# A six-sweep graph kernel on one core: DVE operands in PSUM, groups written out, indices resident, one-hots built in both orientations

## The chip, the cores and the metric

The kernel runs on one core of a Trainium2 chip, in float32 (some one-hots in bfloat16). The metric is the device time of one execution in microseconds, the lower the better: the median of three runs of the kernel before is 7284.38 us. The engines are named as in the profile: PE (TensorE matmul), PEld (its weight loads), DVE (VectorE), ACT (ScalarE), POOL (GpSimd) and SP (SyncE, which here issues only DMAs).

## What is computed

A graph has 3125 nodes with 128 channels and 100000 edges, sorted by destination. Six message-passing layers run one after the other, each over all edges:

```python
e = leaky_relu(el[src] + er[dst])              # L0, GAT, 8 heads: no vectors of the destination
alpha = (q[dst] * (k[src] + e_edge)).sum(c)    # L1, twice, 4 heads; e_edge = edge_attr @ We
alpha = (q[dst] * k[src]).sum(c)               # L2, 4 heads
e = (att * leaky_relu(xl[src] + xr[dst], 0.2)).sum(c)   # L3, twice, 8 heads
p = exp(alpha - segment_max(alpha, dst)[dst])
out = segment_sum(p * v[src], dst) / segment_sum(p, dst)
```

L0 also makes the edge attributes of L1: cos(relative time * Wt + bt) in 64 channels beside 64 given ones. Between the layers stand projections, norms, a feed-forward part and residual sums per node.

## The kernel before

`edge_sweep` runs once per layer, with the kinds "gat", "tconv" (twice), "mha" and "gatv2" (twice). Edges lie in tiles of 128, one edge per partition; 8 tiles are a group, and a sweep has 98 groups (the last has 6 tiles with edges and 2 of padding). Buffers are rings of S = 4 slots (`rows`, `qwin`, `neg`, `part`).

For each group POOL issues 8 indirect DMAs (`gather`, L739), one per tile, each of which fetches 128 rows of the source node's table (1 KB a row in tconv and mha, 512 B in gatv2, 576 B in gat) into `rows`, with its indices read from `idx`, which ACT has cast from `src_col` (L760). POOL's only waits are for `idx` and for the messages of the group four earlier. SP loads 8 windows of 128 destination rows (`qwin`, L674), the marks for the segment maxima (`neg`, L678) and, in tconv, the edge attributes (L680), and stores the partial sums (`part_tab`, L703), 8 runs of 544 or 576 bytes per partition.

A tile's destinations are numbered by rank within the tile. `hot` is the one-hot [edge, rank] and `hot_t` its transpose. In gat and mha DVE builds the one-hot (L981); in tconv and gatv2 ACT does (L780: |rank - column| tile by tile, L791: relu(1 - gap)). PE transposes it (L883), ACT copies it out of PSUM to `hot_t` (L766) and, outside gat, casts `hot_b` to `hot` (L774). PE spreads the destination rows over the edges with `hot_t` (L902, and L899 for edge attributes), DVE forms the scores (`scores`: L1030 adds the edge term to k and v, L1040 multiplies; in gatv2 L1033 adds, L1036 is the slope as max(0.2x, x), L1037 multiplies by att; L1042 reduces), PE transposes the scores (L917), DVE takes running maxima in two scans (L988, L992) and the difference (L997), ACT takes the exponent (L798), PE transposes maxima and weights back (L909, L910), ACT copies them to SBUF as `pm` (L804), and DVE forms the messages (L1070, L1071, L1075). PE sums them per rank (L928) and ACT copies the sums out (L810). In gat DVE also makes angles for the cosines (`angles`, L1051 to L1061), ACT the cosine (L818), PE and ACT turn the attributes (L943, L826) and SP stores them.

The order on each engine is written by hand in a `body` per engine; each calls the steps of neighbouring groups (group i's scores with group i-1's maxima and messages and group i-2's sums). `bodies` writes out the first 8 bodies, loops over those of groups 8 to 91 four at a time and writes out the rest:

```python
for i, k, u in ring[:FIRST]:
    body(i, k, u, i)
with eng.Fori(2, LAST // S) as j:
```

After a sweep, `node_stage` gathers the last rank's row of each tile (7 indirect DMAs at L1108, of which 6 start while the sweep drains), carries sums over tiles that share a node, loads and stores back the first row of each tile (`first`), gathers each node's own row (26 at L1325, POOL, one for each of NB = 26 blocks of 128 nodes), does the node work, projects, and scatters the q rows (26 at L1335) behind the products. The setup has 26 indirect gathers of its own (L356). NB is twice ceil(3125/256), so the last block holds no node.

## Time and profile before

| | |
|---|---|
| median of 3 runs | 7284.38 us (7284.37 to 7298.89) |
| the profiled execution: its span, first to last instruction | 7290.4 us |
| instructions | 132506 |
| busy: PE, DVE, ACT, POOL | 65%, 67%, 56%, 71% |
| mean DMA rate over the span | 183 GB/s |

The profiled execution has no time of its own beside its span; the span lies between the lowest and the highest of the three runs. Times in the rows are microseconds from the start of the span unless they are marked ns. Of an instruction group a row gives line, engine, operation, output<-inputs, shapes and count, then the busy time and the mean duration of one in ns, then the idle time of the engine just before them and what ended it ("issue": nothing that the profile shows). An input or output called bank lies in PSUM; all other tiles lie in SBUF.

### The profile page before, as it was taken

The numbers are of one execution on the slowest core, as the hardware profiler recorded it, in microseconds if no ns is written. First come the engines' busy times: TensorE is split into PE (matmuls) and PEld (weight loads), VectorE is DVE, ScalarE is ACT, GpSimd is POOL, SyncE is SP. The second block draws the span as 40 slices with busy tenths as digits, with TensorE's granted clock in tenths as the row PEclk, the third lists the DMA queues.
The fourth block names the chain that finished last, engine by engine and source line by source line (L and its number), as shares of the span: only waits on it lengthen the run. The fifth ranks groups of instructions, "written<-read, shape, count | busy, mean of one in ns | idle before, by whom it ended". The sixth has DMA issues, their size and how long they took to land. (4 is left out here: it accounts for less than half of the span.)

```text
span 7290.4 us, 132506 instructions
## 1 busy us (share of the span) xinstructions
PE 4733.5 (65%) x30647; PEld 4262.1 (58%) x30647; DVE 4893.6 (67%) x9144; ACT 4079.6 (56%) x9739; POOL 5179.0 (71%) x5105
## 2 busy tenths in 40 slices
PE   2777776577777567777746666645666654666663
PEld 2677775466767457777635565535555553555553
DVE  5777886467777557777655555546777765777776
ACT  1555554466766457667623333326767654767672
POOL 4777774377777577777657777757777766777774
PEclk6777787788888778888868778867888876888886
DMA  2677775289998578898847777735555553555553
GB/s 71 183 192 194 194 196 157 69 251 258 259 261 256 154 219 258 255 261 255 228 116 208 206 203 206 206 102 148 159 159 159 159 139 97 159 159 159 159 159 88
DMA packets 1717674, 1334.47 MB, mean 183 GB/s; under 512 B 384948, under 2 KB 1559891, under 8 KB 1717524
## 3 DMA queue, kind: packets, MB, share of 16 engines
q1 hardware_dynamic: 1516788, 837.31, 40.0%
q0 software_dynamic: 200736, 495.45, 24.8%
q8 instruction: 59, 0.97, 0.1%
q14 instruction: 91, 0.75, 0.0%
HBM read 913.26 MB, written 418.79 MB: 183 GB/s over the span
## 5 line engine op out<-in xcount | busy, mean ns | idle before, releaser
L739 POOL DMA_INDIRECT s_rows<-kv_tab,s_idx x2352 | 2359.8, 1003 | 737.3 <-issue 703.8
L739 POOL DMA_INDIRECT s_rows<-xl_tab,s_idx x1568 | 1622.5, 1035 | 491.6 <-issue 476.8
L902 PE MATMUL bank<-s_qwin,s_hot_t 128*128 128x128 f32 (+1 forms) x9408 | 1657.2, 342 | 12.9 <-ACT s_hot_t L766 7.1
L928 PE MATMUL bank<-s_msg,s_hot 128*128 128x144 f32 (+1 forms) x9408 | 1553.5, 313 | 126.1 <-ACT s_part L810 90.9
L902 PEld LDWEIGHTS bank<-s_qwin,s_hot_t 128*128 128x128 f32 x9408 | 1557.9, 256 | 57.0 <-issue 31.0
L928 PEld LDWEIGHTS bank<-s_msg,s_hot 128*128 128x128 f32 x9408 | 1351.1, 211 | 189.0 <-ACT s_part L810 145.1
L917 PE MATMUL bank<-ident,s_alpha 128*32 128x128 f32 (+1 forms) x588 | 182.6, 310 | 1512.8 <-DVE s_alpha L1042 1506.1
L810 ACT ACTIVATE s_part<-bank 128x288 f32<-128x288 f32 (+1 forms) x2352 | 901.2, 403 | 352.5 <-PE bank L928 299.7
L917 PEld LDWEIGHTS bank<-ident,s_alpha 128*32 128x32 f32 (+1 forms) x588 | 62.6, 107 | 1598.6 <-issue 1598.4
L780 ACT ACTIVATE s_gap<-iota_free,rank_col 128x128 bf16<-128x128 f32 x3136 | 989.5, 387 | 0.1
L798 ACT ACTIVATE s_prob<-s_diff 32x128 f32<-32x128 f32 (+1 forms) x588 | 180.3, 307 | 1436.2 <-DVE s_diff L997 1407.5
L739 POOL DMA_INDIRECT s_rows<-gat_tab,s_idx x784 | 803.7, 1025 | 243.5 <-issue 238.6
L766 ACT ACTIVATE s_hot_t<-bank 128x1024 f32<-128x1024 bf16 (+1 forms) x686 | 605.4, 897 | 535.1 <-PE bank L883 514.8
L1030 DVE TENSOR_TENSOR s_rows<-s_rows,bank 128x1024 f32<-128x1024 f32 x392 | 476.6, 1216 | 593.6 <-DMA s_rows<-kv_tab,s_idx 437.9
L1071 DVE TENSOR_TENSOR s_msg<-s_rows,s_pm 128x1024 f32<-128x1024 f32 x588 | 716.4, 1218 | 0.0
L1040 DVE TENSOR_TENSOR s_prod<-bank,s_rows 128x512 f32<-128x512 f32 x588 | 405.4, 689 | 438.2 <-DMA s_rows<-kv_tab,s_idx 424.7
L1042 DVE TENSOR_REDUCE s_alpha<-s_prod 128x16 f32<-128x512 f32 (+1 forms) x980 | 672.1, 686 | 33.4
L1033 DVE TENSOR_TENSOR s_prod<-bank,s_rows 128x512 f32<-128x512 f32 x392 | 268.8, 686 | 577.6 <-DMA s_rows<-xl_tab,s_idx 577.6
L899 PE MATMUL bank<-We,s_attr_t 128*128 128x128 f32 x3136 | 548.7, 331 | 29.6 <-DMA s_attr_t<-attr_tab 12.2
L899 PEld LDWEIGHTS bank<-We,s_attr_t 128*128 128x128 f32 x3136 | 495.9, 241 | 69.2 <-issue 69.2
L774 ACT ACTIVATE s_hot<-s_hot_b 128x1024 f32<-128x1024 bf16 x490 | 513.6, 1048 | 0.0
L791 ACT ACTIVATE s_hot_b<-s_gap,one 128x1024 bf16<-128x1024 bf16 x392 | 450.1, 1148 | 24.4 <-ACT s_gap L780 14.2
(292 smaller groups left out, 6193.9 us busy)
## 6 DMA issues: line engine op xcount, KB each, us to landing
s_qwin<-q_tab SPq DMA_DIRECT2D x3920, 64.0 KB
part_tab<-s_part SPq DMA_DIRECT2D x294, 576.0 KB
part_tab<-s_part SPq DMA_DIRECT2D x294, 544.0 KB
s_attr_t<-attr_tab SPq DMA_DIRECT2D x196, 512.0 KB
attr_tab<-s_attr_t SPq DMA_DIRECT2D x98, 512.0 KB
s_rows<-kv_tab,s_idx POOLq DMA_INDIRECT x2352
s_rows<-xl_tab,s_idx POOLq DMA_INDIRECT x1568
s_attr<-in_edge_attr SPq DMA_DIRECT2D x97, 256.0 KB
```

The lines of the kernel that those rows point to most:

```text
L739: pool.indirect_dma_start(out=rows[u][:, t, :], out_offset=None, in_=tab, in_offset=bass.IndirectOffsetOnAxis(ap=idx[u][:, t:t + 1], axis= ...
L766: ins = act.activation(hot_t[:, h * per:(h + 1) * per, :], bank[:, 0:per * P].rearrange("p (t e) -> p t e", t=per), ACT.Copy)
L774: act.activation(hot[u][:, :, :], hot_b[u % 2][:, :, :], ACT.Copy).then_inc(hot_cast, 1)
L780: ins = act.activation(gap[:, t, :], pl.iota_free[:, :], ACT.Abs, scale=-1.0, bias=pl.rank_col[:, bass.ds(i * G + t, 1)])
L791: act.activation(hot_b[u % 2][:, :, :], gap[:, :, :], ACT.Relu, scale=-1.0, bias=pl.one[:, 0:1]).then_inc(hot_built, 1)
L810: act.activation(part[u][:, PAIR * c:PAIR * (c + 1), :], part_ps[c % 2][:, 0:PAIR * W].rearrange("p (t w) -> p t w", t=PAIR), ACT.Copy).th ...
L899: pe.matmul(e_ps[h][:, (t - h * per) * D:(t - h * per + 1) * D], attr_t[u][:, t * P:(t + 1) * P], w["We"][:, :], start=True, stop=True)
L902: ins = pe.matmul(q_ps[h][:, (t - h * per) * QW:(t - h * per + 1) * QW], hot_t[:, t, :], qwin[u][:, t, :], start=True, stop=True)
L928: ins = pe.matmul(part_ps[c % 2][:, t * W:(t + 1) * W], hot[u][:, PAIR * c + t, :], msg[:, PAIR * c + t, :], start=True, stop=True)
L1030: v.tensor_tensor(kv, kv, bc(e.unsqueeze(2), [P, HALF, 2, D]), ALU.add).then_inc(e_used, 1)
L1042: v.tensor_reduce(alpha[:, t0:t1, :], prod[h][:, :, :].rearrange("p t (h c) -> p t h c", c=C), AX.X, ALU.add).then_inc(alpha_done, 1)
L1071: v.tensor_tensor(msg[:, :, 0:D].rearrange("p t (h c) -> p t h c", c=C), vals.rearrange("p t (h c) -> p t h c", c=C), bc(p.unsqueeze(3), [ ...
```

## The change

1. PSUM operands. DVE instructions that read two SBUF tensors now read one of them from PSUM: the ramp of `build_hot`, Wt, bt and att are copied once per sweep into bank 0; `messages` reads weights and maxima where PE has transposed them (the copy `pm` goes); the result of the first scan stays in PSUM; the angles are kept in PSUM.
2. The loop goes: all 98 groups are written out on every engine. The last group gathers 6 tiles.
3. Indices resident: `src_col` is int32 and POOL reads it directly; `idx` and its cast go.
4. The partial sums are stored in one run of 4352 or 4608 bytes per partition, so that the rows of a tile are interleaved with those of the group's 7 others. Row numbers in `part_i` and `tile_last_i` are computed accordingly; the first rows of the tiles are loaded in 10 DMAs instead of 2 and, joined, are stored into rows of their own behind the table.
5. One-hots in both orientations: DVE builds `hot` (float32) in every kind; ACT builds `hot_t` from the ranks of the group, broadcast over the partitions (bfloat16, a new 256 KB load per group), in two instructions of 1024 elements. PE's transposes of the one-hot, their copy and cast go.
6. In gatv2 DVE adds into PSUM in place, ACT scales by 0.2 into `prod` (`slopes`), DVE takes the maximum of both. In gat the fold to -|a| moves from DVE to ACT (`folds`).
7. `msg` is double-buffered; PE spreads the first half of the next group ahead of turning the scores; NB is 25.

The diff, cut to its core:

```diff
-        self.src_col = sb("src_col", [P, TB * P])
+        self.src_col = sb("src_col", [P, TB * P], I32)
...
+        self.rank_tab = dram("rank_tab", [TB * P, P], BF16)
...
-        self.part_tab = {H: dram(f"part_tab{H}", [TT * P, D + 2 * H]) for H in (8, 4)}
+        self.part_tab = {H: dram(f"part_tab{H}", [TT * P + TT, D + 2 * H]) for H in (8, 4)}
...
-            for i, k, u in ring[:FIRST]:
+            for i, k, u in ring[:NG + 3]:
                 body(i, k, u, i)
-            with eng.Fori(2, LAST // S) as j:
-                for u in range(S):
-                    body(j * S + u, j, u, FIRST + u)
-            for i, k, u in ring[LAST:]:
-                body(i, k, u, i)
...
+            return pl.last_tiles if n == NG - 1 else G
...
+                    if n >= S:
+                        wait(sp, gap_done, i - S + 1)
+                    sp.dma_start(ranks[u][:, :], pl.rank_tab[i * G:(i + 1) * G, :].rearrange("t e -> (t e)").partition_broadcast(P)
+                                 ).then_inc(ranks_loaded[u], 16)
...
-                    out = part_tab[bass.ds(i * (G * P), G * P), :].rearrange("(t p) w -> p t w", p=P)
-                    sp.dma_start(out, part[u][:, :, :]).then_inc(part_stored[u], 16)
+                    out = part_tab[bass.ds(i * (G * P), G * P), :].rearrange("(p t) w -> p (t w)", t=G)
+                    sp.dma_start(out, part[u][:, :, :].rearrange("p t w -> p (t w)")).then_inc(part_stored[u], 16)
...
-                    wait(pool, idx_ready, i + 1)
...
-                    for t in range(G):
+                    for t in range(tiles_of(n)):
                         pool.indirect_dma_start(out=rows[u][:, t, :], out_offset=None, in_=tab,
-                                                in_offset=bass.IndirectOffsetOnAxis(ap=idx[u][:, t:t + 1], axis=0)
+                                                in_offset=bass.IndirectOffsetOnAxis(
+                                                    ap=pl.src_col[:, i * G + t:i * G + t + 1], axis=0)
...
+                def build_hot_t(i, k, u, n):
+                    wait(act, ranks_loaded[u], 16 * (k + 1))
...
+                        wait(act, hot_t_built, i)
+                    act.activation(gap[:, :], ranks[u][:, :], ACT.Abs, bias=pl.minus_id[:, 0:1]).then_inc(gap_done, 1)
                     wait(act, gap_done, i + 1)
...
+                        wait(act, q_done, QB * (i - 1))
+                    act.activation(hot_t[u % 2][:, :], gap[:, :], ACT.Relu, scale=-1.0, bias=pl.one[:, 0:1]
+                                   ).then_inc(hot_t_built, 1)
...
+                def slopes(i, k, u, n, h):
+                    wait(act, summed, 2 * i + h + 1)
+                    if n >= 1:
+                        wait(act, alpha_done, 2 * (i - 1) + h + 1)
+                    act.activation(prod[h][:, :, :], q_ps[h][:, :].rearrange("p (t d) -> p t d", t=HALF), ACT.Copy, scale=0.2
+                                   ).then_inc(sloped, 1)
...
+                def folds(i, k, u, n):
+                    wait(act, angle_done, i + 1)
+                    act.activation(ang2[u][:, :, :], ang2[u][:, :, :], ACT.Abs).then_inc(folded, 1)
...
+                    if has(n, 2):
+                        build_hot_t(*near(*g, 2))
...
+                def spread(i, k, u, n, h):
+                    per = G // QB
+                    if h == 0:
+                        wait(pe, hot_t_built, i + 1)
+                        wait(pe, q_loaded[u], 16 * G * (k + 1))
...
                     if n >= 1:
-                        wait(pe, prob_copied, i)
+                        wait(pe, msg_done, 3 * i)
...
-                    if has(n, 1):
-                        turn_hot(*near(*g, 1))
...
+                    if QB == 2 and has(n, 1):
+                        spread(*near(*g, 1), 0)
...
+                        spread(*near(*g, 1), QB - 1)
...
-                            wait(v, part_done, NPAIR * (i - S + 1))
-                    elif n >= 2:
...
-                    v.tensor_tensor(out[:, :, :], bc(pl.iota_free[:, :].unsqueeze(1), [P, G, P]),
+                    if n >= S:
+                        wait(v, part_done, NPAIR * (i - S + 1))
+                    v.tensor_tensor(hot[u][:, :, :], bc(iota_ps.unsqueeze(1), [P, G, P]),
                                     bc(pl.rank_col[:, bass.ds(i * G, G)].unsqueeze(2), [P, G, P]),
                                     ALU.is_equal).then_inc(hot_built, 1)
...
+                    v.tensor_tensor_scan(fwd, neg[u][:, 0:P], alpha_t, 0.0, ALU.add, ALU.max).then_inc(fwd_done, 1)
...
+                        v.tensor_tensor(q, q, rows[u][:, h * HALF:(h + 1) * HALF, :], ALU.add).then_inc(summed, 1)
...
+                        wait(v, sloped, 2 * i + h + 1)
+                        v.tensor_tensor(prod[h][:, :, :], q, prod[h][:, :, :], ALU.max).then_inc(q_used, 1)
+                        wait(v, q_used, 2 * i + h + 1)
+                        then(v.tensor_tensor(prod[h][:, :, :], prod[h][:, :, :], bc(att_ps.unsqueeze(1), [P, HALF, D]),
+                                             ALU.mult))
...
                     then(v.tensor_tensor(ang[:, :, :], bc(rel[:, :].unsqueeze(2), [P, G, 64]),
-                                         bc(w["Wt"][:, :].unsqueeze(1), [P, G, 64]), ALU.mult))
-                    then(v.tensor_tensor(ang[:, :, :], ang[:, :, :], bc(w["bt"][:, :].unsqueeze(1), [P, G, 64]), ALU.add))
+                                         bc(Wt_ps.unsqueeze(1), [P, G, 64]), ALU.mult))
+                    then(v.tensor_tensor(a3, ang[:, :, :], bc(bt_ps.unsqueeze(1), [P, G, 64]), ALU.add))
                     then(v.tensor_scalar(tn, a, float(1 / (2 * np.pi)), MAGIC, ALU.mult, ALU.add))
                     then(v.tensor_scalar(tn, tn, MAGIC, None, ALU.subtract))
                     then(v.scalar_tensor_tensor(a, tn, -TWO_PI_HIGH, a, ALU.mult, ALU.add))
-                    then(v.scalar_tensor_tensor(a, tn, -TWO_PI_LOW, a, ALU.mult, ALU.add))
...
-                    v.scalar_tensor_tensor(ang2[u][:, :, :].rearrange(fl), a, -1.0, a, ALU.mult, ALU.min
+                    v.scalar_tensor_tensor(ang2[u][:, :, :].rearrange(fl), tn, -TWO_PI_LOW, a, ALU.mult, ALU.add
...
-                    wait(v, prob_copied, i + 1)
-                    if n >= 1:
-                        wait(v, part_done, NPAIR * i)
+                    out = msg[u % 2]
+                    wait(v, prob_turned, i + 1)
+                    if n >= 2:
+                        wait(v, part_done, NPAIR * (i - 1))
...
-                    p = pm[:, 0:R].rearrange("p (t h) -> p t h", h=H)
-                    v.tensor_copy(msg[:, :, D:D + H], p).then_inc(msg_done, 1)
...
-                    v.tensor_tensor(msg[:, :, D + H:W], pm[:, R:2 * R].rearrange("p (t h) -> p t h", h=H),
+                    v.tensor_tensor(out[:, :, D + H:W], max_ps.rearrange("p (t h) -> p t h", h=H),
...
+                        if has(n, -1):
+                            messages(*near(*g, -1))
+                        if has(n):
+                            scores_gat(*g)
+                    else:
+                        if kind == "gatv2" and has(n):
+                            sums(*g)
+                        if has(n):
+                            for h in range(2):
+                                scores(*g, h)
+                        if has(n, -1):
+                            messages(*near(*g, -1))
+                    if has(n):
+                        build_hot(*g)
...
+                ins = v.tensor_copy(iota_ps, pl.iota_free[:, :])
...
+                    ins = v.tensor_copy(att_ps, w["att"][:, :])
...
+                    for t in range(G):
+                        rows_t = rank0[0:full_tiles // G, t, :].rearrange("(g n) w -> n g w", n=P // G)
+                        sp.dma_start(first[t:P:G, 0:full_blocks, :], rows_t).then_inc(firsts_loaded, 16)
...
+                    sp.dma_start(joined_rows[0:full_tiles, :].rearrange("(g p) w -> p g w", p=P),
+                                 first[:, 0:full_blocks, :]).then_inc(firsts_stored, 16)
...
```

## Rows read from the trace of the kernel before

**Rows 1.** The page, its head and busy times: engine, busy us, share, instructions.

```profile
span 7290.4 us, 132506 instructions
...
PE 4733.5 (65%) x30647; PEld 4262.1 (58%) x30647; DVE 4893.6 (67%) x9144; ACT 4079.6 (56%) x9739; POOL 5179.0 (71%) x5105
```

**Rows 2.** Groups of instructions by line, engine POOL: the gathers and scatters.

```profile
L739 POOL DMA_INDIRECT s_rows<-kv_tab,s_idx x2352 | 2359.8, 1003 | 737.3 <-issue 703.8 <-ACT s_idx L760 33.4
L739 POOL DMA_INDIRECT s_rows<-xl_tab,s_idx x1568 | 1622.5, 1035 | 491.6 <-issue 476.8 <-ACT s_idx L760 14.9
L739 POOL DMA_INDIRECT s_rows<-gat_tab,s_idx x784 | 803.7, 1025 | 243.5 <-issue 238.6 <-ACT s_idx L760 4.8
L1325 POOL DMA_INDIRECT s_own<-part_tab,part_i x156 | 156.5, 1003 | 276.8 <-DMA part_tab<-s_first 231.1 <-issue 45.7
L1335 POOL DMA_INDIRECT q_tab<-s_q_rows,compact_i x130 | 128.1, 985 | 125.1 <-DVE res L1670 91.3 <-issue 22.6 <-DVE s_q_rows L1670 4.9
```

**Rows 3.** Timeline, POOL, written-out start of a sweep: start us, us, instruction [idle before].

```profile
4929.28 0.96 POOL L739 DMA_INDIRECT s_rows<-xl_tab,s_idx  x1 [0.30 <-issue]
...
4939.29 0.94 POOL L739 DMA_INDIRECT s_rows<-xl_tab,s_idx  x1 [0.30 <-issue]
```

**Rows 4.** Sweeps (gat, tconv, mha, gatv2): length; PE, PEld, DVE, ACT, POOL busy; PEclk, DMA share, GB/s.

```profile
158.95:1201.31 1042.36, 787.51 (x4913) 746.57 (x4913) 819.03 (x1643) 591.91 (x1243) 803.72 (x784) 0.76 0.71 190
1435.65:2458.18 1022.53, 763.68 (x5704) 704.26 (x5705) 721.06 (x1160) 707.15 (x1744) 783.99 (x784) 0.86 0.89 256
...
3761.92:4791.60 1029.68, 667.15 (x4177) 607.62 (x4178) 592.88 (x1065) 379.64 (x869) 791.08 (x784) 0.80 0.72 204
4927.99:5978.90 1050.91, 666.25 (x4170) 605.26 (x4171) 757.01 (x1355) 729.78 (x1746) 812.17 (x784) 0.81 0.56 157
...
sum 6217.76, PE 4323.38 PEld 3982.59 DVE 4368.45 ACT 3844.88 POOL 4785.93; mean PE 720.56 PEld 663.76 DVE 728.08 ACT 640.81 POOL 797.66
```

**Rows 5.** Timeline, all engines, tconv loop.

```profile
2003.17 0.95 POOL L739 DMA_INDIRECT s_rows<-kv_tab,s_idx  x1 [0.30 <-issue]
2003.22 1.21 DVE L1030 TENSOR_TENSOR s_rows<-s_rows,bank 128x1024 f32<-128x1024 f32 x1
...
2006.08 1.22 DVE L1071 TENSOR_TENSOR s_msg<-s_rows,s_pm 128x1024 f32<-128x1024 f32 x1
...
2006.92 1.21 POOL L739 DMA_INDIRECT s_rows<-kv_tab,s_idx  x1 [0.30 <-issue]
```

**Rows 6.** Timeline, all engines, gatv2 loop.

```profile
5508.94 0.69 DVE L1036 SCALAR_TENSOR_TENSOR s_prod<-s_prod 128x512 f32<-128x512 f32 x1
5509.21 1.24 POOL L739 DMA_INDIRECT s_rows<-xl_tab,s_idx  x1 [0.30 <-issue]
```

**Rows 7.** Timeline, all engines, gat loop.

```profile
400.68 0.43 DVE L1055 TENSOR_SCALAR s_turns<-s_ang 128x512 f32<-128x512 f32 x1
...
401.04 0.94 POOL L739 DMA_INDIRECT s_rows<-gat_tab,s_idx  x1 [0.30 <-issue]
401.14 0.43 DVE L1056 TENSOR_SCALAR s_turns<-s_turns 128x512 f32<-128x512 f32 x1
```

**Rows 8.** Groups by line, DVE and ACT: the one-hot, a step of gat, a copy out of PSUM.

```profile
L981 DVE TENSOR_TENSOR s_hot_b<-iota_free,rank_col 128x1024 bf16<-128x1024 f32 x98 | 119.3, 1218 | 16.1 <-PEq L1245 16.1
...
L826 ACT ACTIVATE s_attr_t<-bank 128x512 f32<-128x512 f32 x196 | 106.0, 599 | 0.4 <-PE bank L943 0.4
...
L1055 DVE TENSOR_SCALAR s_turns<-s_ang 128x512 f32<-128x512 f32 x98 | 41.9, 427 | 3.3
```

**Rows 9.** Timeline, hand-over from a node stage to a sweep.

```profile
2596.00 0.41 ACT L760 ACTIVATE s_idx<-src_col 128x8 int32<-128x8 f32 x3 [25.16 <-PEq L1245]
...
2597.04 0.99 POOL L739 DMA_INDIRECT s_rows<-kv_tab,s_idx  x1 [7.12 <-ACT s_idx L760]
```

**Rows 10.** DMA view of 1500 to 2400 us (tconv): queue, packets, MB, share of 16 engines.

```profile
q1 hardware_dynamic: 204749, 141.15, 54.6%
q0 software_dynamic: 33222, 90.77, 35.4%
```

327 lines of the change are left out of this document (136 added, 191 removed).

## The prediction, on record before the changed kernel ran

> **What bounds the kernel now.** The page says 71% for POOL and 65 to 67% for PE and DVE [rows 1], which names no bound. The groups of POOL do: the 4704 gathers of the six sweeps were busy for 2359.8 + 1622.5 + 803.7 = 4786.0 us, and of the 1472.4 us of idle time before them 1419.2 ended by "issue", that is 0.30 us before each, and only 53.1 by anything that POOL waited for, all of it ahead of a sweep's first gathers [rows 2]. So POOL issues gathers back to back from a sweep's start to its end, and DVE, PE and ACT wait for rows. The sweep lengths agree: from the first gather's start to the last one's end they sum to 6217.8 us [rows 4], of which gathers and issue gaps make 4786.0 + 1419.2 = 6205.2.
>
> What does one gather take? Where DVE rests, at the start of a sweep, eight periods last 4939.29 - 4929.28 = 10.01 us, 1.251 each [rows 3]. In the sweeps the mean is 6217.8 / 4704 = 1.322. The mean duration differs by kind, 1003 ns for kv, 1025 for gat, 1035 for xl [rows 2], although a kv row has twice the bytes of an xl row: size does not explain it. The timeline does. In tconv a gather that starts at 2003.17, beside L1030, takes 0.95; one that starts at 2006.92, while L1071 runs (2006.08 to 2007.30), takes 1.21 [rows 5]. In gatv2 a gather that starts at 5509.21 inside L1036 (5508.94 to 5509.63) takes 1.24 [rows 6]. L1071 and L1036 read two SBUF operands, L1030 reads one SBUF and one PSUM operand. The delay fits "the gather needs something about 0.12 us after its start, and gets it when the DVE instruction ends": 2007.30 - 2006.92 - 0.12 = 0.26 and 5509.63 - 5509.21 - 0.12 = 0.30, as measured over 0.945. What all this costs is 6217.8 - 4704 x 1.251 = 333 us, the largest thing that the change can touch.
>
> **The change, part by part.**
>
> PSUM operands. In tconv, mha and gatv2 no DVE instruction of the sweep that lasts over 0.3 us still reads two SBUF tensors: L1071, L981, L1036, L1037 and L992 either go or take one operand from PSUM. I take the whole 333 us: -333. From both sides: 0, if the delay has another cause; -333, if all goes. Nearest row: L1030, no delay [rows 5]. In gat L1056 stays SBUF to SBUF with a single input. The gather at 401.04 runs beside the end of L1055 (to 401.11) and through L1056, and takes 0.94 [rows 7], so I charge 0. The Trainium skill (GPSIMD Engine Reference, Specifications) says that POOL's SBUF interface conflicts with DVE instructions that have two SBUF inputs and also with those in a 2-port mode; by its second half L1056 would still delay the gathers that start in it, at most 98 x 0.43 = 42 us. For the two-input half the trace agrees, for the other it does not.
>
> Last group. Two gathers less per sweep, 12 x 1.251 = -15. Sweeps: 6 x 782 x 1.251 = 5870 us instead of 6218, -348 in all.
>
> Written-out groups. POOL's gaps are 0.30 us in the part that is written out already [rows 3] and in the loop [rows 5, 6], so the loop costs POOL nothing and its removal brings nothing: 0. What could come is stalls while code is loaded; the written-out start shows none on POOL. The Trainium skill (Advanced Engine Details and Errata, ISA Cache) gives 256 instructions to a line and two lines; by it all the written-out code is fetched once. Rows 3 lie in such code.
>
> Indices resident. At a sweep's start ACT begins the casts at 2596.00 and POOL gathers at 2597.04 [rows 9]: 1.0 us of waiting goes per sweep, -6 in all (bounds 0 and -6). Inside the sweep POOL did not wait for indices, 0. POOL's remaining wait, for the messages of the group four back, has about 10 us of slack, since they are formed while the gather three further on runs.
>
> NB 25. One own-row gather and one scatter less in each of 6 stages, one search in the setup: 13 x 1.25 = 16 us of POOL at 1003 and 985 ns a piece plus the issue gap [rows 2]. Most stand in back-to-back runs that end a stage: I take -14 (0 to -16). The 8 more loads of first rows per stage go out on SP at the stage's start and are needed only behind the transposes, scans and spreads of the carry: 0 under that cover; without it at most one gather period each, 8 x 1.25 x 6 = +60. The setup's new row arithmetic, some ten DVE instructions of a few columns: +2.
>
> Work that moves. It costs time only if an engine then needs more than 8 x 1.251 = 10.01 us per group. DVE needed 757.01 / 98 = 7.72 in gatv2, 721.06 / 98 = 7.36 in tconv, 592.88 / 98 = 6.05 in mha, 819.03 / 98 = 8.36 in gat [rows 4]. tconv and gatv2 gain one `build_hot`, 1.22 [rows 8]: 8.58 and 8.94. In gatv2 the count of other steps stays (add, max, multiply, reduce). In gat a step of 0.69 goes, and L1055, 0.43 now [rows 8], reads PSUM, at most as long as a two-input step, 0.69: 7.9 to 8.4. The Trainium skill (VectorE: DVE Perf Modes, Why PSUM operands drop a tier) has such a single-input step lose its double rate; that is the upper of these two values, and covered. For writing into PSUM from DVE no row exists; I bound it by 0 and by +0.3 us for each of the two adds, which still gives 9.5. The new wait in gatv2 (DVE for `slopes`): ACT's copy of that size takes 0.60 [rows 8] and the second add, 0.69, covers the first half's; behind DVE's wait stand messages and build_hot, and up to 0.3 us may show, 9.2 to 9.8 in all. ACT falls from 729.78 / 98 = 7.4 [rows 4] by thirteen instructions and gets four; PE loses eight transposes per group. SP gets one more issue per group, past which the marks are moved; they are needed two groups later. The tail of a sweep gets one build_hot ahead of the last maxima, 1.2, and loses the copy of the weights: 0 within 7 us over all.
>
> DMA. tconv uses 0.89 of the engines at 10.43 us per group [rows 4], 9.28 us. The ranks add 256 KB per group; at 256 / 0.89 = 288 GB/s that is 0.91, in sum 10.19 if nothing else changed, 0.18 over POOL's 10.01. But the part stores, 1024 pieces of 544 bytes for each of the stretch's 900 / 10.43 = 86 groups, are 88064 of the 204749 packets of q1 and 48 of its 141 MB [rows 10]; in one run per partition they need a fraction of the packets. Saving 0.2 us of 9.28 is enough. I take 0 (bounds 0 and +35, or +80 if the engines are loaded unevenly). The other kinds stand at 0.56 to 0.72 [rows 4].
>
> Sum: -348 - 6 - 14 + 2 = -366. The profiled span is 7290.4 and goes to 6924; it stands 6.0 above the median of the runs, 7284.4, which goes to 6918. I say **6920**. An effect of 0.2%, 15 us, is about what a measurement of this kernel can tell from none.
>
> **The rivals.**
> - DMA engines bind tconv. For it: 10.19 against 10.01. Against it: the fewer packets. +35 to +80 us, 6955 to 7000. Chance 0.17.
> - DVE binds gatv2, through PSUM writes and the wait for `slopes`, at 10.4 instead of 10.01: 196 x 0.4 = +78, about 7000. For it: only 1.07 us of room. Against it: each wait has a cover. Chance 0.09.
> - By the skill's rule for 2-port modes, gat keeps part of its delay. As a mechanism here: a start falls into L1056 in 8 x 0.43 / 10.01 = 0.34 of the groups for 0.2 us on average, +7 us; at most +42: 6927 to 6962. Rows 7 speak against it. Chance 0.04.
> - The change doesn't do what it says: gathers are delayed by DVE activity whatever the operands. Then -15 - 6 - 14 + 2, 7251. Rows 5 speak against it. Chance 0.04.
> - Slower: in tconv and gatv2 DVE carries out in order a body in which each hand-over (PE's spread, ACT's slopes, the turned weights) is waited for. It decides from 366 / 392 = 0.93 us over 10.01, a period of 10.94: 2.0 us of waits in gatv2 and 2.4 in tconv. At 11.5 us it gives 392 x 1.49 - 366 = +218, 7500. Now DVE's only long wait is for rows. Chance 0.04.
>
> **How the numbers follow.** The forecast has 0.62, and the skill's rival, counted apart, lies in the same range, 6890 to 6962. From the sum of the favourable bounds and a shorter tail comes 6885 as the low end; the high end takes in both partial rivals and part of an uncovered first-row load: 7030. Left out are the last two rivals and what is below, under 0.2. Faster by over 0.2%: 0.95; within: 0.01; slower: 0.04.
>
> **What would show it.** Right: gathers of 0.94 to 0.95 us throughout, their mean under 0.96 in each kind; six sweeps of about 978 us; POOL's idle time by "issue" alone; DVE 8.6 to 9.0 us busy per group in tconv and gatv2; DMA share in tconv 0.90 to 0.97. Wrong: long gathers beside DVE instructions with a PSUM operand (the mechanism); idle time of POOL that ends by a message on DVE (DVE or DMA binds); gaps on DVE, PE and ACT together without a releaser (code loading); node stages no shorter than now.

## The result, and the profile after

The changed kernel takes 7059.07 us, the median of four runs (7057.57 to 7061.33); beside them the kernel before took 7291.64 (7284.37 to 7306.88). The ratio is 0.968, interval 0.966 to 0.969: 3.2% faster. The forecast was 6920, its range ended at 7030. So the direction was right and the size was not: of the 366 us expected some 230 came.

The page of the changed kernel, head and busy times, in answer to [rows 1]:

```profile
span 7058.2 us, 100657 instructions
...
PE 4367.5 (62%) x25901; PEld 3913.4 (55%) x25901; DVE 5261.5 (75%) x9430; ACT 3157.8 (45%) x5509; POOL 4812.4 (68%) x5080
```

The groups of POOL, to be held against [rows 2] (line, operation, tiles, count | busy us, mean ns | idle time before them and what ended it):

```profile
L760 POOL DMA_INDIRECT s_rows<-kv_tab,src_col x2346 | 2218.7, 946 | 733.9 <-issue 688.3 <-DVE s_msg L1057 25.6 <-POOLq L1242 20.0
L760 POOL DMA_INDIRECT s_rows<-xl_tab,src_col x1564 | 1476.3, 944 | 489.4 <-issue 443.5 <-DVE s_msg L1057 32.6 <-POOLq L1242 13.3
L760 POOL DMA_INDIRECT s_rows<-gat_tab,src_col x782 | 739.8, 946 | 390.4 <-issue 236.3 <-DVE s_msg L1057 149.7 <-POOLq L1242 4.4
```

In [rows 2] a gather took 1003, 1035 and 1025 ns by kind; here it takes 946, 944 and 946, whatever the row's size. In kv and xl the idle time is still 0.31 us before each gather, the price of issuing one (where messages are named there, they had come within it). In gat 390.4 - 782 x 0.305 = 152 us are more than that, and they end by the messages. That is the miss. The six sweeps, from the first gather's start to the last one's end, show it at a glance (columns as in [rows 4]):

```profile
157.10:1282.90 1125.80, 691.61 (x4051) 631.19 (x4051) 762.65 (x1524) 711.79 (x1124) 739.77 (x782) 0.68 0.71 197
1520.20:2497.80 977.60, 710.34 (x4925) 662.55 (x4926) 823.34 (x1249) 403.89 (x673) 739.58 (x782) 0.88 0.92 295
2631.30:3608.90 977.60, 710.19 (x4904) 662.07 (x4904) 821.50 (x1249) 400.16 (x669) 739.59 (x782) 0.87 0.93 294
3747.40:4724.80 977.40, 620.76 (x3383) 561.31 (x3384) 592.90 (x1063) 398.38 (x673) 739.43 (x782) 0.74 0.80 242
4855.50:5831.70 976.20, 606.11 (x3368) 551.90 (x3368) 855.04 (x1447) 500.47 (x867) 738.10 (x782) 0.77 0.67 196
5966.70:6942.90 976.20, 607.95 (x3368) 553.40 (x3368) 854.07 (x1444) 500.92 (x867) 738.13 (x782) 0.77 0.67 196
```

Five sweeps last 976 to 978 us, as forecast (978). The first, gat, lasts 1125.8: 148 more than forecast, and 83 more than the 1042.4 it took before. Outside the sweeps the span has 1047.4 us, 25 less than before. The forecast's missing 140 us all lie in gat. What is POOL waiting for there? The waits of 300 to 1100 us (us in total, times, longest):

```profile
DVE s_msg L1052 <- PE bank L888: 223.7, 42, 7.5
PE bank L919 <- ACT s_attr L819: 217.4, 33, 7.7
ACT s_gap L783 <- DMA s_ranks<-rank_tab: 177.5, 34, 7.0
...
POOL s_rows L760 <- DVE s_msg L1057: 123.7, 37, 5.0
```

and of the same stretch the waits on SyncE's queue:

```profile
SPq L729 <- ACT s_attr_t L826: 192.1, 42, 6.5
```

Read upwards: POOL waits for DVE's messages, DVE for PE's turned weights, PE for ACT's cosines, ACT for the ranks that SP loads, and SP for ACT's copy of the turned attributes. Each of them waits in about every second group and none is busy: ACT 711.79 of 1125.80 us, DVE 762.65. It is a closed loop. The timeline of one turn (start us, us, instruction [idle before]), in three extracts from one stretch of the trace:

```profile
612.28 0.33 SPq L729 DMA_DIRECT2D attr_tab<-s_attr_t  x1
612.66 0.43 SPq L725 DMA_DIRECT2D part_tab<-s_part  x1
...
614.87 4.45 SPq L692 DMA_DIRECT2D s_qwin<-er_tab  x8
...
619.41 0.38 SPq L697 DMA_DIRECT2D s_ranks<-rank_tab  x1
...
624.02 1.15 ACT L783 ACTIVATE s_gap<-s_ranks,minus_id 128x1024 bf16<-128x1024 bf16 x1 [6.36 <-DMA s_ranks<-rank_tab]
```

```profile
627.40 1.28 ACT L819 ACT_TABLE_LOAD   x1
...
628.70 1.33 ACT L819 ACTIVATE s_attr<-s_ang,half_pi 128x512 f32<-128x512 f32 x2
...
630.05 1.28 ACT L794 ACT_TABLE_LOAD   x1
...
632.14 0.58 ACT L826 ACTIVATE s_attr_t<-bank 128x512 f32<-128x512 f32 x1
632.28 0.22 DVE L1052 COPY s_msg<-bank 128x64 f32<-128x64 f32 x1 [6.81 <-PE bank L888]
...
634.55 0.94 POOL L760 DMA_INDIRECT s_rows<-gat_tab,src_col  x1 [3.48 <-DVE s_msg L1057]
635.35 0.60 ACT L826 ACTIVATE s_attr_t<-bank 128x512 f32<-128x512 f32 x1 [0.44 <-PE bank L919]
...
635.97 0.33 SPq L729 DMA_DIRECT2D attr_tab<-s_attr_t  x1
```

SP comes to the store of the attributes and has to wait for the copy until 612.28. Only then can it issue the other store, load the row numbers of the eight windows into registers (1.5 us, some 0.6 of it a wait for PE), issue the windows and, behind them, the ranks (619.41): 7.1 us. The ranks land and ACT starts on them at 624.02: 4.6 us. ACT builds `hot_t`, folds, loads the table, takes two cosines until 630.03: 6.0 us. Then it loads the other table, takes the exponent and copies while PE turns, and the second copy ends at 635.95, when SP's store goes out: 5.9 us. In sum 23.7 us for two groups, where POOL needs 16 x 1.251 = 20.0. Over the whole sweep it is 1125.8 / 49 = 23.0.

### The profile page after: what moved, and what is told of

The parts are those of the page before. It is cut to its first block and busy times, and to the rows that moved or that the text cites. A ratio compares the mean times of both kernels' runs of the same rounds, so it can differ in the third digit from the quotient of the medians.

```text
span 7058.2 us, 100657 instructions
## 1 busy us (share of the span) xinstructions
PE 4367.5 (62%) x25901; PEld 3913.4 (55%) x25901; DVE 5261.5 (75%) x9430; ACT 3157.8 (45%) x5509; POOL 4812.4 (68%) x5080
## 5 line engine op out<-in xcount | busy, mean ns | idle before, releaser
L760 POOL DMA_INDIRECT s_rows<-kv_tab,src_col x2346 | 2218.7, 946 | 733.9 <-issue 688.3
L905 PE MATMUL bank<-s_msg,s_hot 128*128 128x144 f32 (+1 forms) x9408 | 1770.3, 344 | 299.5 <-ACT s_part L800 280.9
L760 POOL DMA_INDIRECT s_rows<-xl_tab,src_col x1564 | 1476.3, 944 | 489.4 <-issue 443.5
L783 ACT ACTIVATE s_gap<-s_ranks,minus_id 128x1024 bf16<-128x1024 bf16 x588 | 673.1, 1145 | 982.4 <-DMA s_ranks<-rank_tab 980.5
L760 POOL DMA_INDIRECT s_rows<-gat_tab,src_col x782 | 739.8, 946 | 390.4 <-issue 236.3
L953 DVE TENSOR_TENSOR s_hot<-bank,rank_col 128x1024 f32<-128x1024 f32 x588 | 714.7, 1215 | 0.0
L1053 DVE TENSOR_TENSOR s_msg<-s_rows,bank 128x1024 f32<-128x1024 f32 x588 | 711.6, 1210 | 0.0
L1022 DVE TENSOR_REDUCE s_alpha<-s_prod 128x16 f32<-128x512 f32 (+1 forms) x980 | 672.4, 686 | 33.6
L1020 DVE TENSOR_TENSOR s_prod<-bank,s_rows 128x512 f32<-128x512 f32 x588 | 405.6, 690 | 384.7 <-DMA s_rows<-kv_tab,src_col 357.4
L787 ACT ACTIVATE s_hot_t<-s_gap,one 128x1024 f32<-128x1024 bf16 x588 | 675.1, 1148 | 19.3
L997 DVE TENSOR_TENSOR bank<-bank,s_rows 128x512 f32<-128x512 f32 x392 | 253.9, 692 | 166.1 <-DMA s_rows<-xl_tab,src_col 138.3
```

The costliest lines, as they stand in the source:

```text
L760: pool.indirect_dma_start(out=rows[u][:, t, :], out_offset=None, in_=tab, in_offset=bass.IndirectOffsetOnAxis(ap=pl.src_col[:, i * G + t:i ...
L783: act.activation(gap[:, :], ranks[u][:, :], ACT.Abs, bias=pl.minus_id[:, 0:1]).then_inc(gap_done, 1)
L787: act.activation(hot_t[u % 2][:, :], gap[:, :], ACT.Relu, scale=-1.0, bias=pl.one[:, 0:1]).then_inc(hot_t_built, 1)
L905: ins = pe.matmul(part_ps[c % 2][:, t * W:(t + 1) * W], hot[u][:, PAIR * c + t, :], msg[u % 2][:, PAIR * c + t, :], start=True, stop=True)
L953: v.tensor_tensor(hot[u][:, :, :], bc(iota_ps.unsqueeze(1), [P, G, P]), bc(pl.rank_col[:, bass.ds(i * G, G)].unsqueeze(2), [P, G, P]), ALU ...
L1020: v.tensor_tensor(prod[h][:, :, :], q, rows[u][:, t0:t1, 0:D], ALU.mult).then_inc(q_used, 1)
```

## The experiments

**1. The ranks one group earlier (e1_ranks_early).**

```diff
+                def load_ranks(i, k, u, n):
+                    if n >= S:
+                        wait(sp, gap_done, i - S + 1)
+                    sp.dma_start(ranks[u][:, :], ...).then_inc(ranks_loaded[u], 16)
...
-                    if n >= S:
-                        wait(sp, gap_done, i - S + 1)
-                    sp.dma_start(ranks[u][:, :], ...).then_inc(ranks_loaded[u], 16)
+                    if kind != "gat":
+                        load_ranks(i, k, u, n)
...
                 def body(*g):
...
+                    if kind == "gat" and has(n, 3):
+                        load_ranks(*near(*g, 3))
                     if has(n, 2):
                         load(*near(*g, 2))
...
```

> The changed kernel with one edit in the GAT layer: SyncE issues the load of a group's ranks one group earlier, ahead of the eight window loads, of the store of the turned attributes and of the store of the parts; nothing else moves. Theory A (a loop over the queues: the ranks come late because their DMA is issued behind stores that wait for ScalarE's copies; the ReLU build of the transposed one-hots waits for them about 6.4 us in every second group, and the cosines, TensorE's turns, the messages and the gathers behind them wait in turn): ScalarE's wait for the ranks (177.5 us between 300 and 1100) goes to under 20, the first sweep falls from 1125.8 us to 978 to 1000, and the time from 7059 to 6910 to 6940. Theory B (ScalarE's own work and its order in the GAT layer set 11.5 us per group, the late load only fills slack): the wait for the ranks goes, and the sweep stays above 1090, the time above 7025. Theory C (TensorE turns the attributes through one bank, in step with ScalarE's copies): as B, and the wait of TensorE for the copies or the cosines takes the place.

Measured: 6902.05 us (6900.63 to 6904.10), 0.947 of the kernel before (0.946 to 0.949), 8 us under the range that theory A gave. The first two sweeps:

```profile
157.20:1136.60 979.40, 731.22 (x4112) 668.38 (x4112) 772.33 (x1542) 733.70 (x1146) 741.24 (x782) 0.73 0.81 228
1361.60:2339.20 977.60, 707.30 (x4914) 659.42 (x4915) 823.09 (x1249) 403.32 (x672) 739.57 (x782) 0.89 0.92 294
```

The gat sweep lasts 979.4 us, and ACT does the work of 1125 us in it, 733.70 us busy: its own work was no bound (theory B), nor was the single bank (theory C). ACT's wait for the ranks is gone from the list, and SP's longest one is left at a tenth:

```profile
SPq L733 <- ACT s_attr_t L835: 18.6, 11, 3.4
```

Theory A holds. One DMA, issued one body too late, cost 157 us, 2.2% of the kernel.

**2. The cosines ahead of the one-hots (e2_cos_first).**

```diff
-                    if has(n, 2):
-                        build_hot_t(*near(*g, 2))
                     if kind == "gat" and u % 2 == 0:
...
+                    if has(n, 2):
+                        build_hot_t(*near(*g, 2))
```

> The changed kernel with one edit in the GAT layer: in ScalarE's order of a group the folds and cosines of two groups stand ahead of the build of the transposed one-hots of group n + 2 (after it before), so that late ranks no longer hold the cosines. Theory A (the late load of the ranks holds the cosines): the chain over the cosines is cut, but the one-hots come later, behind two folds, two cosines and a table load, and TensorE's spread and the scores with them; the sweep falls to between 978 and 1080 us. Theory B (ScalarE's total work sets the pace, order and loads do not): the sweep stays within 20 us of 1125.8. Theory C (TensorE and ScalarE in step over the one bank of turned attributes): within 20 us of 1125.8 too, with TensorE's wait for the cosines (217.4 us between 300 and 1100) gone and its wait for the copies in its place.

Measured: 6918.89 us, ratio 0.950 (0.948 to 0.951), gat sweep 987.6. The ranks stand where they stood in SP's order, but what waits for them is no longer ahead of the cosines (ACT's wait for them between 300 and 1100 falls from 177.5 to 71.2 us). Cutting the loop at ACT is worth nearly what cutting it at SP is; B and C fall again.

**3. No table loads (e4_no_tables).** The cosine becomes a scaled copy, so the time encodings are not computed.

```diff
-  attr[u][:, :, 0:64], ang2[u][:, :, :], ACT.Sin, scale=-1.0, bias=pl.half_pi[:, 0:1]
+  attr[u][:, :, 0:64], ang2[u][:, :, :], ACT.Copy, scale=-1.0
```

> The changed kernel with the cosine of the GAT layer's time encoding replaced by a scaled copy, so the encodings are not computed and the edge attributes differ; what it takes from the time is ScalarE's two table loads per two groups (about 1.3 us each) and nothing else of note. Theory A (late ranks): ScalarE has slack, so the sweep changes by less than the tables' 1.3 us per group at full, and ScalarE still waits for the ranks; the sweep stays above 1060 us. Theory B (ScalarE's own work sets the pace): the sweep falls by the whole 1.3 us per group, some 98 x 1.3 = 127 us, to about 1000.

Measured in one run: 6926.98 us, gat sweep 998.4. By what I had written this speaks for B. But ACT still waited for the ranks, 212.7 us in 57 waits between 300 and 1100:

```profile
ACT s_gap L783 <- DMA s_ranks<-rank_tab: 212.7, 57, 7.6
```

An engine whose own work sets the pace does not wait a quarter of its time. The expectation of theory A was badly drawn: the table loads lie on the loop as well, so what they take comes off each turn. Two of them, 1.28 us each as the timeline shows, leave 22.98 - 2.56 = 20.4 us for two groups, and 998.4 / 49 = 20.4. A loop is shortened by any of its links, which is why a single such run cannot name the cause.

**4. The store one body later (e6_store_later, three times).** SP stores the attributes of group n - 4 instead of n - 3, when ACT's copy is long done.

```diff
-                    if kind == "gat" and has(n, -3):
-                        store_attr(*near(*g, -3))
+                    if kind == "gat" and has(n, -4):
+                        store_attr(*near(*g, -4))
...
```

> The changed kernel with one edit in the GAT layer: SyncE stores the turned attributes of a group one body later (of group n - 4 instead of n - 3), so that ScalarE's copy is long done when SyncE comes to the store; the ranks stay behind the window loads. The loop theory: the link from ScalarE's copy back to SyncE is cut, nothing else holds the ranks, and the GAT sweep falls to 978 to 1000 us, the time to 6900 to 6925. Rivals: the store of the parts, which waits for ScalarE's copies of group n - 2 in the same place, takes over the link, and the sweep stays between 1040 and 1126; or ScalarE's copy of group n - 1 has to wait for the later store, which would show as ScalarE's wait for the DMA of the attributes.

> The kernel of e6_store_later again, on another chip. Loop theory: the GAT sweep 978 to 1000 us, the time 6900 to 6925. Rival (the store of the parts takes over the link): sweep 1040 to 1126, time 6980 to 7060.

> The kernel of e6_store_later a third time. Where the kernel before takes about 7290 us, the loop theory expects the GAT sweep at 978 to 1000 us and the time at 6900 to 6925; the rival (the store of the parts takes over the link to ScalarE) a sweep of 1040 to 1126 and a time of 6980 to 7060.

The first two (9915.06 and 9840.30 us) fell on chips on which the kernel before itself took 9958 to 10095 us, and so did all runs of experiments 5, 7, 8 and 9. Their times say nothing of the pace; single instructions on the engines last as long as elsewhere. The third, where the kernel before took 7297.0: 6966.82 us, gat sweep 1035.8, two groups in 21.1. SP's waits are now

```profile
SPq L725 <- ACT s_part L802: 160.4, 59, 4.2
```

Both ranges were missed, the rival's by little (1040 to 1126 for the sweep, 6980 to 7060 for the time), and its mechanism is what the waits show: with the one store out of the way SP waits for ACT at the next, the store of the parts, and 58 of the 148 us of loss stay, two fifths. What holds the ranks back is their place behind any store that waits for ACT. Moving the load (experiment 1) removes all of it, moving one store does not.

**5. The ranks ahead of the windows (e5_ranks_ahead, four times)**, to see whether 4 us of issuing are enough of the loop.

```diff
                 def load(i, k, u, n):
                     if n >= S:
+                        wait(sp, gap_done, i - S + 1)
+                    sp.dma_start(ranks[u][:, :], ...).then_inc(ranks_loaded[u], 16)
+                    if n >= S:
                         wait(sp, q_done, (i - S + 1) * QB)
...
-                    if n >= S:
-                        wait(sp, gap_done, i - S + 1)
-                    sp.dma_start(ranks[u][:, :], ...).then_inc(ranks_loaded[u], 16)
```

> The changed kernel with one edit: in SyncE's load of a group the ranks come ahead of the eight window loads instead of behind them; they still stand behind the two stores of the body before, which wait for ScalarE. The loop theory so far (in two groups of 23.7 us an unbroken chain runs store of the turned attributes, window loads, ranks, one-hots, cosines, turn, copy, store; every microsecond cut out of it comes off the two groups, down to POOL's 20.0): the eight window issues take about 4 us of it, so the GAT sweep falls to the floor or just above it, 978 to 1010 us, and the time to 6905 to 6945. Rival (the ranks are late because of the stores' waits alone, the window issues run beside them): the sweep stays above 1090, the time above 7025.

> The kernel of e5_ranks_ahead again, on another chip (the first ran where the kernel before itself took 10074 us). Loop theory: the GAT sweep 978 to 1010 us, the time 6905 to 6945. Rival (the stores' waits alone make the ranks late): sweep above 1090, time above 7025.

> The kernel of e5_ranks_ahead a third time; on the two chips before, the kernel before itself took over 9950 us. Where the kernel before takes about 7290 us, the loop theory expects the GAT sweep at 978 to 1010 us and the time at 6905 to 6945; the rival (the stores' waits alone make the ranks late) a sweep above 1090 and a time above 7025.

> The kernel of e5_ranks_ahead a fourth time (the three before fell on chips where the kernel before took over 9950 us). e6_store_later_3 brought the GAT sweep to 1035.8 us, with SyncE now waiting 160 us for ScalarE at the store of the parts: the loop closes over either store. Loop theory: the window issues are 4.0 us of the 23.7 us loop, so with the ranks ahead of them the loop is 19.7 us, just under POOL's 20.0, and the GAT sweep is 978 to 1010 us, the time 6905 to 6945. Rival (the stores' waits alone make the ranks late): a sweep above 1090, a time above 7025.

Measured: 9894.36 us with the kernel before at 10074.11; 9720.37 (9958.19); 9879.37 (10095.15); 9764.31 (9959.97). The gat sweep took 1345 to 1371 us, against 1371 and 1364 in kernels whose gat is that of the change (e7_two_port and its repeat, on the first two of these chips, where the sweeps here took 1361 and 1345): nothing can be told from it. Whether this smaller move is enough stays open. What these traces show to be slow is SyncE: its instructions come at steps of 0.70 or 1.40 us for 3000 to 3300 us of the span (some 130 us in the trace of the changed kernel), and the issue of eight windows takes 8.42 us at 5201.82 of e6_store_later, where its median in the changed kernel is 4.1. Why, I did not pursue.

**6. Two operands back in SBUF (e3_iota_sbuf)**: the test of the mechanism on which the 333 us rested.

```diff
-  bc(iota_ps.unsqueeze(1), [P, G, P])
+  bc(pl.iota_free[:, :].unsqueeze(1), [P, G, P])
...
-  bc(att_ps.unsqueeze(1), [P, HALF, D])
+  bc(w["att"][:, :].unsqueeze(1), [P, HALF, D])
```

> The changed kernel with two operands put back into SBUF: the ramp that the build of the one-hots compares with, in all three kinds of layer, and the attention vector of the two GATv2 layers. Theory of contention (a gather that VectorE's instruction of two SBUF operands overtakes within some 0.1 us is held until that instruction ends): the build of the one-hots (1215 ns) catches one gather in eight or so where it falls at random, and where it sits at the end of VectorE's group it meets gathers that wait for no one; the mean gather rises from 946 ns to 955 to 1010 in the kinds where it is caught, the tconv and MHA sweeps grow by 8 to 50 us each, the GATv2 sweeps by 15 to 100 each since two further products per group are of two SBUF operands, and the time by 60 to 250 us. Rival (the gather period fell because the operands' banks or the written-out groups changed the timing, not because of the SBUF operands): gathers stay at 944 to 948 ns and the time within 10 us of 7059.

Measured: 7310.24 us (7302.66 to 7312.55), 1.003 of the kernel before (1.002 to 1.004). The whole gain of the change is gone, and more; the time and the means of xl and gat lie a little above the ranges given. POOL's gathers:

```profile
L760 POOL DMA_INDIRECT s_rows<-kv_tab,src_col x2346 | 2340.5, 998 | 733.9 <-issue 693.8 <-DVE s_msg L1057 20.1 <-POOLq L1242 20.0
L760 POOL DMA_INDIRECT s_rows<-xl_tab,src_col x1564 | 1606.6, 1027 | 489.4 <-issue 466.4 <-POOLq L1242 13.3 <-DVE s_msg L1057 9.8
L760 POOL DMA_INDIRECT s_rows<-gat_tab,src_col x782 | 792.5, 1013 | 344.0 <-issue 224.4 <-DVE s_msg L1057 115.2 <-POOLq L1242 4.4
```

Against the change that is 2340.5 - 2218.7 + 1606.6 - 1476.3 + 792.5 - 739.8 = 305 us of longer gathers, of which gat, bound by its loop, passes on only 6 (sweep 1132.0). The other five sweeps grow by 33 to 66 each. And one caught gather, in MHA:

```profile
4007.21 1.22 DVE L953 TENSOR_TENSOR s_hot<-iota_free,rank_col 128x1024 f32<-128x1024 f32 x1
...
4007.50 1.74 POOL L760 DMA_INDIRECT s_rows<-kv_tab,src_col  x1 [0.30 <-DVE s_msg L1057]
```

L953 ends at 4008.43; 4008.43 - 4007.50 - 0.12 = 0.81, and 1.74 - 0.81 = 0.93, the length of an undisturbed one. The rule of the prediction, "about 0.12 us after its start, until the DVE instruction ends", gives the case to 0.02. The instruction itself takes as long as from PSUM (1216 against 1215 ns): the move to PSUM buys nothing for DVE and everything for POOL.

**7. A long instruction with one SBUF input (e7_two_port, twice)**, added in MHA alone behind the build of the one-hots. It computes nothing of use.

```diff
+                    if kind == "mha" and has(n):
+                        v.wait_ge(spared, g[0] + 1)
+                        v.tensor_scalar(spare_b[:, :], spare_a[:, :], 1.0, None, ALU.subtract).then_inc(spared, 1)
...
```

> The changed kernel with one VectorE instruction per group added in the MHA layer alone, behind the build of the one-hots: a subtraction of a constant over 128 x 1536 elements from one spare SBUF tile to another (one input, no PSUM), about 1.3 us, which computes nothing of use; VectorE has the room (6.0 us busy of 10.0). It stands where the two-operand build stood in the run with the ramp in SBUF, which lengthened this layer's sweep by 48 us. If only instructions with two SBUF inputs delay the gathers: the sweep stays at 977 to 979 us, gathers at 946 ns, the time within 8 us of 7059. If an instruction in the double-rate form delays them too, as the Trainium skill (GPSIMD Engine Reference, Specifications) has it: the sweep grows by 30 to 60 us and the mean gather to 980 to 1010 ns in this layer.

> The kernel of e7_two_port again, on another chip. On the first, 96 of the 782 gathers of the MHA layer took over 980 ns and their mean was 993 ns, so the long single-input instruction does delay gathers. Then here: mean gather of 985 to 1000 ns in the MHA layer alone, that sweep 1010 to 1025 us instead of 977.4, the time 7090 to 7110. Rival (only two SBUF inputs delay; the first chip's own disturbance made those gathers long): 946 ns, 977 to 979 us, 7050 to 7067.

Measured: 9841.32 us (before: 10074.11) and 9741.93 (9958.19), so the sweep's growth can't be read (at 1314.0 and 1294.4 us mha is even shorter than in the kernels without the instruction on such chips, 1353 to 1399), but the gathers can. In the second run, the mha sweep and, for comparison, a tconv sweep of the same kernel:

```profile
L763 POOL DMA_INDIRECT s_rows<-kv_tab,src_col x782 | 777.0, 994 | 525.8 <-DVE s_msg L1060 280.6 <-issue 236.7 <-POOLq L1250 8.5
```

```profile
L763 POOL DMA_INDIRECT s_rows<-kv_tab,src_col x782 | 740.8, 947 | 782.6 <-DVE s_msg L1060 548.7 <-issue 225.9 <-POOLq L1250 8.0
```

777.0 - 740.8 = 36 us of longer gathers, 96 of them over 0.98 us in 98 groups, in both runs. So one input is enough if the instruction is of the double-rate form (1536 elements in 0.95 us, where the 1024 of L953 take 1.22). At the single rate one input does nothing: L1022, which reads one SBUF tile of 512 elements in 686 ns, had 361 gathers start inside it in the last five sweeps of the changed kernel, and the longest took 0.96 us. Two of its encounters:

```profile
5104.25 1.33 POOL L763 DMA_INDIRECT s_rows<-kv_tab,src_col  x1 [16.12 <-DVE s_msg L1060]
5104.51 0.95 DVE L1090 TENSOR_SCALAR s_spare_b<-s_spare_a 128x1536 f32<-128x1536 f32 x1
...
5111.55 1.06 DVE L1090 TENSOR_SCALAR s_spare_b<-s_spare_a 128x1536 f32<-128x1536 f32 x1
...
5112.14 1.29 POOL L763 DMA_INDIRECT s_rows<-kv_tab,src_col  x1 [0.30 <-issue]
```

In the first the gather had started 0.26 us earlier, was past its first need, and still ended 0.12 us after L1090 did. So it needs the thing a second time, near its end. In the second DVE's instruction took 1.06 instead of 0.95: it began in the last third of the gather before and was itself held, and then held the next gather (5112.61 - 5112.14 - 0.12 = 0.35, and 0.94 + 0.35 = 1.29).

Only the double-rate form holds a gather at its second need. In experiment 6, where L953 reads two SBUF operands, a gather that came first ran through to its end inside it:

```profile
4386.47 0.94 POOL L760 DMA_INDIRECT s_rows<-kv_tab,src_col  x1 [0.30 <-issue]
...
4386.77 1.22 DVE L953 TENSOR_TENSOR s_hot<-iota_free,rank_col 128x1024 f32<-128x1024 f32 x1
```

There are 390 such gathers in that trace, and the longest took 0.96 us. Of the 96 long gathers of e7_two_port_2, 49 ended 0.12 us after L1090, like the one at 5104.25, and 47 were held at the first need.

The Trainium skill (GPSIMD Engine Reference, Specifications) states this conflict for the 2-port modes, and the rows agree. It also says (SBUF — State Buffer, Who interferes with whom) that whichever of the two issues first has the ports and the other blocks. Here both sides were seen to wait, but the gather only at two moments, not from its start.

**8. The parts in eight pieces (e8_eight_pieces, four times)**, with the row numbers left as they are, so that later gathers read other rows.

```diff
-  out = part_tab[...].rearrange("(p t) w -> p (t w)", t=G)
+  out = part_tab[...].rearrange("(t p) w -> p t w", p=P)
```

> The changed kernel with the partial sums of a group stored in eight pieces of 544 or 576 bytes per partition, as in the kernel before, in all layers; the row numbers stay those of the changed kernel, so that later gathers read other rows (the output is not computed) and only the time of the store is told. If the store in one run is what keeps the DMA engines under POOL's pace in the tconv layers (10.19 us of DMA per group against 10.01 by the estimate in the prediction): the tconv sweeps grow from 977.6 to 995 to 1020 us each, with POOL's idle time ended by messages or VectorE's by rows, the MHA and GATv2 sweeps stay, and the time rises by 35 to 85 us. If the packets did not matter: all sweeps within 2 us and the time within 10 us of 7059.

> The kernel of e8_eight_pieces again, on another chip; the row numbers stay those of the changed kernel, so that later gathers read other rows. If the store in one run keeps the DMA engines under POOL's pace: the tconv sweeps 995 to 1020 us each, the time up by 35 to 85 us. If the packets did not matter: within 2 us per sweep and 10 us in all.

> The kernel of e8_eight_pieces a third time; the row numbers stay those of the changed kernel, so that later gathers read other rows. Where the kernel before takes about 7290 us: if the store in one run keeps the DMA engines under POOL's pace, the tconv sweeps are 995 to 1020 us each and the time is up by 35 to 85 us; if the packets did not matter, within 2 us per sweep and 10 us in all.

> The kernel of e8_eight_pieces a fourth time; the row numbers stay those of the changed kernel, so that later gathers read other rows. Where the kernel before takes about 7290 us: if the store in one run keeps the DMA engines under POOL's pace, the tconv sweeps are 995 to 1020 us each and the time is up by 35 to 85 us; if the packets did not matter, within 2 us per sweep and 10 us in all.

Measured: 9899.65 us, 9740.04, 9935.11 and 9780.35, all beside a kernel before of 9958 to 10095. No pace can be read, but the work of the DMA engines can: share times length. The first tconv sweep with eight pieces and, from the same chip, with one run per partition (e5_ranks_ahead_2):

```profile
1777.70:3221.20 1443.50, 818.69 (x4877) 747.43 (x4877) 822.17 (x1240) 384.79 (x665) 739.05 (x782) 0.75 0.69 198
```

```profile
1751.40:3206.20 1454.80, 813.61 (x4842) 747.76 (x4842) 814.94 (x1229) 380.23 (x661) 738.96 (x782) 0.74 0.65 196
```

0.69 x 1443.5 / 98 = 10.2 us per group against 0.65 x 1454.8 / 98 = 9.6: the pieces cost about 0.5 us of the 16 engines per group (by the same reckoning 0.3 in the second tconv sweep of this chip, 0.5 and 0.4 on the chip of the first runs). In the changed kernel at its own pace it is 0.925 x 977.6 / 98 = 9.2; with the pieces that would be some 9.7, still under POOL's 10.0. That tconv would have held its pace with the old store is thus likely, and not shown.

**9. The loop back (e10_loop)**: groups 8 to 91 in a loop of four again, with the indices cast on ACT, which the loop needs.

```diff
-            for i, k, u in ring[:NG + 3]:
-                body(i, k, u, i)
+            for i, k, u in ring[:FIRST]:
+                body(i, k, u, i)
+            with eng.Fori(2, LAST // S) as j:
+                for u in range(S):
+                    body(j * S + u, j, u, FIRST + u)
+            for i, k, u in ring[LAST:]:
+                body(i, k, u, i)
...
+                    act.activation(idx[u][:, :], pl.src_col[:, bass.ds(i * G, G)], ACT.Copy).then_inc(idx_ready, 1)
```

> The changed kernel with two parts undone together: the loop over groups 8 to 91, four at a time, is back, and so are the casts of the indices on ScalarE (the loop needs them); everything else stays. Prediction's terms: written-out groups 0, indices 6 us at the sweeps' starts. Five sweeps stay within 3 us of 977, the time outside the sweeps rises by up to 6; the GAT sweep, in which ScalarE is on the loop of waits, gains one cast of 0.41 us per group, up to 0.8 us per two groups, up to 40 us. In all 7060 to 7110 us. Rival (the loop's branches and register arithmetic on SyncE, or code fetched again on each turn, cost the groups time): sweeps of tconv, MHA and GATv2 longer by over 5 us each, the time above 7110.

Measured: 10026.90 us beside 9959.97 for the kernel before, and beside 9764 and 9780 for two written-out kernels on the same chip. All six sweeps took between 1436 and 1535 us. The loop gives SyncE, the slow engine there, 3600 to 4200 instructions per sweep instead of 2700 to 3000, so this run is inconclusive for other chips. The traces of the two main kernels say more. In the first tconv sweep the gathers before took 783.99 us [rows 4]; at the 739.58 / 782 = 0.946 us of the changed kernel they take 741.5, and the sweep 1022.53 - 42.5 = 980.0, or 1.250 us for each of 784. The changed kernel has 977.60 / 782 = 1.250. Beside the longer gathers the loop thus cost this sweep nothing, as forecast.

## Why the prediction was wrong, point by point

- **The mechanism of the gathers** was right, and its size: the five sweeps other than gat are at 976 to 978 us (forecast 978), gathers at 944 to 946 ns. Experiment 6 shows it by putting two operands back, which brings back 251 us; for the other operands it is inferred from the mean gather, which is the undisturbed one in every kind. One detail was off. Who waits is settled at the gather's start and not 0.12 us later: in experiment 6 L953 held every gather that started from 0.03 us behind it to 0.15 before its end, and none that started within 0.024 us of it.
- **The step that failed** is "It costs time only if an engine then needs more than 8 x 1.251 = 10.01 us per group", applied to gat by DVE's sum alone (7.9 to 8.4; it came to 762.65 / 98 = 7.8). For gat no load, no order and no hand-over was followed, neither SP's nor ACT's, though the change puts three links there at once: a load of 256 KB, issued behind two stores that wait for ACT; a build on ACT that waits for that load; and the folds and cosines behind this build. No engine was over 8 us per group, and the sweep was bound at 11.5. "SP gets one more issue per group, past which the marks are moved; they are needed two groups later" looked at what the new issue delays, not at what delays the new issue.
- **The rival that ended slower** named the right kind of thing, an in-order chain of hand-overs, but in tconv and gatv2 and on DVE, where it did not show. In gat, where it arose, it took back about 150 of the 366 us.
- **Last group, indices, NB 25**: outside the sweeps the span fell by 25 us, forecast 6 + 14 - 2 = 18. The hand-overs between sweeps show it: 133.5 us from the first tconv sweep's last gather to the next sweep's first, 138.9 before [rows 4, 9]. With the early ranks it is 1034.8 outside the sweeps, 12.6 less still, nearly all of it between gat's last gather and the next sweep (225.0 us instead of 237.3).
- **DVE binds gatv2**: no. 855.04 / 98 = 8.7 us per group, and the wait for `slopes` amounts to 37.5 us over 392 halves, 0.1 us each. The groups by line:

```profile
L1015 DVE TENSOR_TENSOR s_prod<-bank,s_prod 128x512 f32<-128x512 f32 x392 | 269.0, 686 | 38.0 <-ACT s_prod L808 37.5 <-issue 0.5
L997 DVE TENSOR_TENSOR bank<-bank,s_rows 128x512 f32<-128x512 f32 x392 | 253.9, 692 | 166.1 <-DMA s_rows<-xl_tab,src_col 138.3 <-PE bank L880 27.1
...
L1037 DVE TENSOR_SCALAR s_turns<-bank 128x512 f32<-128x512 f32 x98 | 67.7, 691 | 3.3
```

  An add that writes into PSUM (L997) takes 692 ns, within the 0.3 us allowed for it. The single-input step of gat that reads PSUM (L1037), 427 ns in [rows 8], takes 691, the upper of the two values given, and the Trainium skill's rule for it (VectorE: DVE Perf Modes, Why PSUM operands drop a tier) holds.
- **DMA binds tconv**: no. The share is 0.92 to 0.93, within the 0.90 to 0.97 given; the estimate of 10.19 us per group for the old store was high by about 0.5.
- **The double-rate rule in gat** was given 0.04 on the strength of [rows 7]. The rule holds (experiment 7), and "for the other it does not" rested on one gather. The gather at 401.04 had started 0.10 us before L1056, so it came first, and L1056 was over at 401.57, 0.53 us after the gather's start and before its second need. The same trace has the conflict from DVE's side: L1056, alike in form and size to L1055 (427 ns), takes 489 on average and 0.57 us in 40 of the 98 groups:

```profile
L1056 DVE TENSOR_SCALAR s_turns<-s_turns 128x512 f32<-128x512 f32 x98 | 47.9, 489 | 3.4
```

In the changed kernel a gather that comes second is delayed:

```profile
599.89 0.43 DVE L1038 TENSOR_SCALAR s_turns<-s_turns 128x512 f32<-128x512 f32 x1
599.98 1.15 POOL L760 DMA_INDIRECT s_rows<-gat_tab,src_col  x1 [0.30 <-issue]
```

600.32 - 599.98 - 0.12 = 0.22, and 1.15 - 0.22 = 0.93. Ten of the 782 gathers are longer than 0.98 us, by 1.5 us in sum, so the price was right and the reason was not.
- **With its one slip mended** (e1_ranks_early) the kernel takes 6902, inside the forecast's own range of 6890 to 6962. It beats both kernels.

## What to carry to other kernels

Where an engine is taken off the critical path, follow for each kind of work the order of the queues as a loop: from a load's issue to its consumer, to the store that waits for the consumer's result, and to the next load that stands behind this store on the same queue. If the turn is longer than the new period, it is the new period, however idle the engines are. A load for which a buffer is free goes ahead of stores that wait. And keep long vector instructions from having two SBUF inputs, or the double-rate form, beside indirect DMAs.
